# Slot-table rows of 512 instead of 64 bytes, with their first contents copied in halves from a block of 512 rows

## What is computed

```python
for k in range(TOP_K):
    y = _dispatch_compute(xf, top_experts[:, k], w1, w2, capacity)
    out = out + y * expert_weights[:, k][:, None]
```

## Time and profile before

| what | before |
|---|---|
| median of 3 executions | 2439.61 us (2436.92 to 2441.55) |
| the profiled execution | 2450.27 us |
| its span, first to last instruction | 2448.5 us |
| mean granted TensorE clock | 0.962 |
| busy: TensorE, VectorE, ScalarE, GpSimd | 90%, 55%, 41%, 47% |
| moved by DMA | 209.40 MB, 86 GB/s over the span |

### The profile page before, as it was taken

One profiled execution on the slowest core, in us unless ns is written; L12 is line 12 of the kernel. 1 busy time (PEld: TensorE's weight loads), 2 busy tenths in 40 slices (PEclk: granted clock), 3 DMA queues, 4 the chain that ended last, 5 costly groups with the idle time before them and its releaser, 6 DMA issues.

```text
span 2448.5 us, 57464 instructions
## 1 busy us (share of the span) xinstructions
PE 2204.8 (90%) x22468; PEld 1919.9 (78%) x22468; DVE 1344.1 (55%) x3312; ACT 1006.4 (41%) x2149; POOL 1142.9 (47%) x911
## 2 busy tenths in 40 slices
PE   6749998999999995999899999729999999999997
PEld 6738887999999995777677777628888899999997
DVE  7745443555555552578677786635444455555552
ACT  4433333444443442446545565423333344344442
POOL 4754766444444433223343333254677544444443
PEclk9999999999999998999999999859999999999999
DMA  8522433434344434101211111223333443433432
GB/s 334 209 72 47 92 73 81 80 96 100 79 97 85 92 75 112 34 24 72 72 38 55 55 72 56 71 78 80 77 79 76 96 98 81 100 78 96 98 82 29
DMA packets 129221, 209.40 MB, mean 86 GB/s; under 512 B 24876, under 2 KB 105328, under 8 KB 122864
## 3 DMA queue, kind: packets, MB, share of 16 engines
q0 software_dynamic: 57344, 69.21, 17.2%
q1 hardware_dynamic: 71696, 137.62, 16.3%
HBM read 136.03 MB, written 72.88 MB: 85 GB/s over the span
## 4 chain that ended last, share of the span: by engine, by line
PE 48%; DVE 4%; issue 3%; another core or an unknown queue 3%; ACT 1%; POOL 1%; DMA 1%; POOLq 0%; DVEq 0%; ACTq 0%
PE bank L630 15%; PE bank L641 14%; PE bank L714 9%; PE bank L802 3%; PE bank L835 1%; PE bank L770 1%; PE bank L619 1%; PE bank L785 1%; PE bank L874 1%; PE bank L820 1%; PE bank L732 1%; POOL slot_table L381 0%; DVE aw L1754 0%; DVE xnl L1728 0%
## 5 line engine op out<-in xcount | busy, mean ns | idle before, releaser
L1096 ACT ACTIVATE h<-bank 128x512 f32<-128x512 f32 x512 | 306.3, 598 | 934.2 <-PE bank L630 775.2
L1663 DVE CAST hh<-h 128x512 fp32r<-128x512 f32 x512 | 223.2, 436 | 776.3 <-ACT h L1096 670.7
L641 PE MATMUL bank<-w2h,hh 128*128 128x256 f32 x2048 | 586.3, 286 | 7.7 <-issue 7.4
L641 PE MATMUL bank<-w2l,hh 128*128 128x256 f32 x2048 | 582.7, 285 | 8.5 <-issue 8.3
L641 PE MATMUL bank<-w2h,hl 128*128 128x256 f32 x2048 | 582.7, 285 | 7.1 <-issue 6.8
L630 PE MATMUL bank<-xh,w1h 128*128 128x512 f32 x1024 | 412.7, 403 | 15.4 <-issue 9.2
L641 PEld LDWEIGHTS bank<-w2h,hh 128*128 128x128 f32 x2048 | 394.1, 192 | 30.1 <-issue 10.8
L641 PEld LDWEIGHTS bank<-w2l,hh 128*128 128x128 f32 x2048 | 394.5, 193 | 28.9 <-issue 11.7
L630 PE MATMUL bank<-xl,w1h 128*128 128x512 f32 x1024 | 409.6, 400 | 0.7 <-issue 0.6
L418 POOL DMA_INDIRECT xe<-xn_rows,tab x256 | 269.5, 1053 | 294.2 <-issue 261.8
L630 PE MATMUL bank<-xh,w1l 128*128 128x512 f32 x1024 | 403.8, 394 | 0.7 <-issue 0.6
(11 more groups left out here) (209 smaller groups left out, 3321.1 us busy)
## 6 DMA issues: line engine op xcount, KB each, us to landing
stg<-in_L_ffn_w SPq DMA_DIRECT2D x64, 1024.0 KB
xb<-acc SPq DMA_DIRECT2D x9, 1024.0 KB, 8.4
xa<-in_L_attn_x SPq DMA_DIRECT2D x8, 1024.0 KB, 14.0
xn_rows<-xa SPq DMA_DIRECT2D x8, 1024.0 KB
xn_rows<-xn_r SPq DMA_DIRECT2D x8, 1024.0 KB, 4.7
xr<-acc SPq DMA_DIRECT2D x7, 1024.0 KB, 5.4
out_rows<-xr SPq DMA_DIRECT2D x7, 1024.0 KB
slot_table<-pay,idx POOLq DMA_INDIRECT x256
```

The lines of the kernel that those rows point to most:

```text
L641: last = pe.matmul(o, a[:, fj, s], c[:, fj, :], start=(fj == 0 and n == 0 and t % 2 == 0), stop=(fj == FJ - 1 and n == 2), skip_group_chec ...
L1096: act.activation(h32[fj % 2][:], bank[fj % 2][:], ACT.Gelu_apprx_tanh).then_inc(f.gelu, 1)
L1663: dve.tensor_copy(hh[:, fj, :], h32[fj % 2][:]).then_inc(f.hh, 1)
```

## The change

A table row is 128 words (512 bytes). The scatter writes the whole row, so its window in `pay` is 128 words too, and the padding grows from 14 to 126 words per batch (the memset of L1596 from 112 to 1008 elements per partition). A table is 8 MB instead of 1. The input `slots_in` is now 512 such rows (256 KB), and a half of a table (the rows of one choice, 4 MB) is filled by one DMA whose source is that block, read 16 times. The first half of table 0 is issued behind the load of x of batch 3; its second half and both halves of table 1 stand in a row behind `normal_store(7)`, ahead of `ffn(0)`. GpSimd waits for the second half of table 0 behind the third gather, and for both halves of table 1 before attention. `tab` keeps two words per row, and the table loads fetch only these.

```diff
-        tab = sb("tab", [P, GE, GT, ROW])
+        tab = sb("tab", [P, GE, GT, 2])
...
+            def empty_slots(r, half, done):
+
+                rows = slot_d[r][half * (SLOTS // 2):(half + 1) * (SLOTS // 2), :].rearrange("(g s) w -> g s w", s=G)
+                sp.dma_start(rows, slots_in.unsqueeze(0).to_broadcast([NG // 2, G, ROW])).then_inc(done, 16)
+
             for b in range(1, B):
                 sp.dma_start(xa[:, b], x_w[b, :, :, :]).then_inc(X0[b], 16)
+                if b == 3:
+                    empty_slots(0, 0, S0.slot0)
...
             biased_store(1)
-            sp.dma_start(slot_d[0], slots_in).then_inc(S0.slot0, 16)
             biased_store(2)
...
             normal_store(7)
-            sp.dma_start(slot_d[1], slots_in).then_inc(S0.slot1, 16)
+            empty_slots(0, 1, S0.slot1)
+            empty_slots(1, 0, S0.slot2)
+            empty_slots(1, 1, S0.slot2)
...
-                tab_t = slot_d[r].rearrange("(g p t) w -> g p t w", p=P, t=GT)
+                tab_t = slot_d[r].rearrange("(g p t) w -> g p t w", p=P, t=GT)[:, :, :, 0:2]
...
                 gather(2, [(f.tab2, 16), (f.xT, 1)])
+                if r == 0:
+                    held(pool, S0.slot1, 16)
...
-            pool.wait_ge(S0.slot1, 16)
+            pool.wait_ge(S0.slot2, 32)
...
-ROW = 16
+ROW = 128
...
-    slots = np.zeros((SLOTS, ROW), np.uint32)
-    slots[:, 0] = N + np.arange(SLOTS) % G
+    slots = np.zeros((G, ROW), np.uint32)
+    slots[:, 0] = N + np.arange(G)
```

More of the change, by code:

```diff
@@ L174, in macaron_kernel @@
         nth = fill_numbers()
-        S0 = sems("setup", "const vec hvec rw zero acc_z out_z xn_z slot0 slot1 rope wraw wT wTh wTl bias memset base passed")
+        S0 = sems("setup", "const vec hvec rw zero acc_z out_z xn_z slot0 slot1 slot2 rope wraw wT wTh wTl bias memset base passed")
         X0 = [ctx.enter_context(nc.semaphore(f"first_x{b}")) for b in range(B)]
```

## The result

The kernel after the change takes 2462.6 us (median of 7 runs, 2452.94 to 2470.94); the kernel before, 2439.61 on the same chip (7 runs, 2421.72 to 2442.44). The ratio is 1.0101, 95% interval 1.0069 to 1.0134: slower by 17 to 33 us. The forecast was 2448.0, a loss of 8.4. The profiled execution of after is at its median (2462.6, span 2460.8), that of before stood 10.7 above its own, so the two traces differ by 12.3 us only.

The account below looks back on a forecast made before the run. TensorE, busy 90% of the span, was taken as the bound, with uncovered waits for gathered tokens at each expert stage's start. Copies 7.6 plus table loads 0.8 gave +8.4 us on the 2439.61 median: 2448.0, range 2395 to 2472.

Parts of the forecast that it names:

- Start-up copy: Table 0's first half, behind the fourth x load: lands near 28 us, gains and costs nothing; first `acc` store has 1.4 slack.
- Three copies ahead of the first table load: Behind `normal_store(7)`: 12.58 MB and queued scatters delay the first table load from 148.92 to 156.5, +7.6 us.
- 12 such pieces: 29.5 us: Ahead of the first expert stage: 12 pieces per ring at 2.46 us each occupy rings from 121.2 to 150.7.
- 20 x 0.23 = 4.6 us: Ring time of 20 scatters of batches 5 to 7 among the copies, half a gather each; rings clear at 155.3.
- The rule that spoke against the change: Trainium skill's 214 GB/s for HBM-to-HBM copies: the three copies before the first expert stage take 59 us, sum near +38.
- Table loads, +0.8: 512 pieces of 8 bytes instead of 128 of 256 add 0.4 us to the first load of either expert stage.
- the other loads lie a whole token group ahead of use: Inside the expert stages: table loads after each stage's first are early enough that narrowing them adds nothing.
- Scatter issue: GpSimd's issue time per scatter hardly depends on row size: 0 taken, between 0 and 0.1 us each.
- the moved wait: GpSimd's wait for the other half after the third gather, and its round-1 wait, find copies long landed: nothing.
- The third rival: Scatters' small writes stretch token groups and attention, some 108 us; whole rows could free part, half giving 2394. Chance 0.24.
- The slow copy: Long shared-source copies run at half rate: 29.5 us more at expert start, 8.4 at the `acc` store, 2486. Chance 0.12.
- The hidden copy: Scatters stay at 0.06 us per ring, table load 4.2 us late; total 2442 to 2445. Chance 0.12.

Follow-up runs that it names:

- the narrow loads alone: Kernel before with only its table loads changed, to two words of each 64-byte row: ratio 1.0091 on chip C, 1.0019 on chip D.
- long source, narrow loads: Changed kernel, each copy reading its own 4 MB input of 8192 rows once instead of 256 KB 16 times: ratio 1.0076 against before.
- scatters of 64 bytes, narrow loads: Changed kernel with 512-byte rows and long copies, but scatters writing only the first 16 words of a row: ratio 1.0082 against before.
- copies spread, narrow loads: Changed kernel, table 0's second half copied behind `normal_store(3)`, table 1's halves in the middle of the first expert stage: ratio 1.0081 against before.
- quarters spread, narrow loads: Changed kernel, table 0's second half cut in four between stores before the first expert stage, table 1 in quarters during attention: ratio 1.0069 against before.
- copies alone, whole loads: Kernel before plus three 4.19 MB copies into tensors nobody reads, behind the copy of table 1: ratio 1.0091 on B, 1.0087 on D.

## Why the prediction was right in direction and short in size

The time of 2462.6 us lies in the stated range (2395 to 2472), but 4.6 above the 2458 at which the forecast's own bounds ended. The path was the predicted one; two terms of the sum were too small.

**Start-up copy, costed at nothing: right.** It landed at 29.4 us (4.38 + 25.0; forecast near 28), `ln_rs` moved to 29.55, nothing earlier came of it. The first `acc` store took longer than its forecast of 40 us, and the slack of 1.4 us at it was used up: VectorE's row of after, against 41.44 in the earlier trace rows,

```profile
42.36 2.29 DVE L1623 TENSOR_TENSOR xr<-xa,hbias 128x2048 f32<-128x2048 f32 x1 [0.38 <-DMA acc<-xr]
```

waits 0.38 us for it, and the last scatter is 0.43 us later; the copies ahead of the table load cover that. Up to 38 us the rings moved 346 GB/s instead of 373 at nearly the same share (0.94 and 0.93), with this copy among their traffic.

**Three copies ahead of the first table load: the failed step.** The mechanism is the predicted one: 12 pieces per ring, the last scatters behind them because a ring turns to the other queue once per packet, and the table load behind these scatters. The term was mis-sized. "12 such pieces: 29.5 us" took some 40 (121.5 to about 161.5, forecast 150.7), because the 2.46 us of the earlier trace rows hold for the first piece on each ring only; later ones take 3.34. "20 x 0.23 = 4.6 us" for the scatters was about 2, for another reason than bytes: 436 packets that had been given no turn. Then some 1.2 us to the load, as forecast. That makes 15.6 us where 7.6 stood; by luck the scatters' term, too large by 2.7, hid a part of the 10.5 that the copies' term was short. Both spread runs show that the delay belongs to the copies at that place: without them there the load is at 148.9.

The rule that spoke against the change, 214 GB/s at full rate for copies of tiles of 128 x 16 KiB between HBM tensors (the Trainium skill, DMA: Bandwidth & Descriptors, Latency and other measured facts), named the right danger and the wrong size for these copies. The 12.6 MB went in 40 us, 315 GB/s, which lies between it and the 426 I used. The Trainium skill also states (same page, Queues, rings and completion order) that a DMA engine turns between its queues after each packet. The trace agrees, with 64 packets of either queue from 132 to 142 us, and what follows is that large pieces on one queue set the pace of the other.

**Table loads, +0.8: right at the place that was costed, too small for the kernel.** Load to gather is 3.06 us instead of 2.55 at the first expert stage (164.53 to 167.59) and 3.04 instead of 2.53 at the second: +1.0 together. But the narrow loads alone cost 3.0 us by medians on D (2.3 to 6.6) and 20 on C. The forecast's "the other loads lie a whole token group ahead of use", which put them at nothing, may be the place, and no run shows it.

**Scatter issue and the moved wait, 0: right.** The page of after, part 5, against the earlier trace rows:

```profile
L389 POOL DMA_INDIRECT slot_table<-pay,idx x256 | 265.7, 1038 | 114.4 <-issue 94.5
```

**The sum.** Start 15.6 and table loads 1.0 are 16.6 us, just under the interval of the ratio (17 to 33) and 6.4 under the medians' 23.0. With the 3.0 us of chip D for the narrow loads it is 18.6. On the chips without stalls these two terms are nearly all. By medians:

| run | chip | late or lost at the named place | whole loss | rest |
|---|---|---|---|---|
| long source, narrow loads | B | 14.5 (first table load) | 17.9 | 3.4 |
| scatters of 64 bytes, narrow loads | B | 15.9 (first table load) | 19.9 | 4.0 |
| copies spread, narrow loads | B | 15.3 (two groups) | 18.0 | 2.7 |
| quarters spread, narrow loads | D | 10.5 (attention) | 13.5 | 3.0 |
| copies alone, whole loads | B | 19.0 (first table load) | 20.6 | 1.6 |
| copies alone, whole loads | D | 18.6 (first table load) | 20.2 | 1.6 |

A place is read in one trace: the first table load against 148.91 on B and 149.32 on D, the two groups against even ones, attention against the narrow loads alone. Each rest alone is within the interval of its ratio; but it is 2.7 to 4.0 us wherever the loads are narrow. On A 4.4 us are left beyond 18.6, on C 7.5 beyond 16.4 and 3.0. The narrow loads may hold them, since alone they cost 20 us on C; but the change, which has them and the copies, costs 27 there and not 40. No run separates them.

**The third rival (small writes stretch the groups, 0.24): fallen, though its pool is real.** I had priced it at 37 + 31 + 40 = 108 us. Chips B and D, with the very same kernel before, are 100 us faster than A, and the three places are those: eight groups in 187.5 us instead of 224.8 in the first stage and 218.9 in the second, and from the last group of the first stage to the second stage's first gather 639 to 644 us (seven kernels, all but the quarters) instead of 682.8. The "remote" waits are not there. Of the 37 us in the first stage TensorE is idle for 19.5 and busy for 17.8 more, at a mean granted clock of 0.95 instead of 1.00. But on A eight groups went only from 224.80 to 216.41 and from 218.86 to 218.18 with whole rows, in one execution each; on C from 226.5 to 224.8 and from 225.1 to 234.0. In attention the six waits of ScalarE stand as they did (before, after, on A):

```profile
ACT vz L1188 <- remote: 40.0, 6, 7.3
```

```profile
ACT vz L1198 <- remote: 39.5, 6, 7.1
```

**The slow copy (0.12)** came true by a third: it wanted 59 us for the three copies, they took 40 and not 29.5. **The hidden copy (0.12)** fell with the load at 164.5.

## What to carry to other kernels

A copy that nobody waits for is not free while its queue is first in, first out: what its ring time exceeds the slack by, it costs to the next load that somebody does wait for. Here 12.6 MB, 40 us on the rings, cost 15.6 us ahead of the first expert stage, 8.4 MB cost 15 in its middle and about 10 in attention. Take the rate for such a copy from a stretch of full rings with the same two ends, not from the first piece of a burst; and mind the size of the pieces, because another queue on the same rings gets one packet per piece. Cutting a load down to the bytes in use isn't free either: 3.0 us on D. Before rows are widened so that writes are large, check that the small ones cost anything: here 8, 64 and 512 bytes made no difference on the chips on which that was measured.

## What the runs showed of the hardware

- The same kernel takes 2337 to 2339 us on two chips and 2440 to 2457 on two others. The difference lies in waits that the profile marks "remote", while GpSimd issues eight scatters and four gathers in a row, and six scatters in attention: ScalarE and VectorE then wait together, and TensorE goes on with gaps marked "issue". On the fast chips these waits are absent. What makes them was not found.
- Copies from HBM to HBM: 2.47 us for the first 64 KB piece on each ring, 3.34 in the long run with a shared source of 256 KB, 3.11 with one of 4 MB. From SBUF to HBM in 2 KB pieces, 348 to 369 GB/s.
- Rings with work of two queues took their packets one for one, whatever their size: 64 and 64 in 10 us, up to 64 KB on one side and 2 KB on the other.
- With full rings, TensorE stood still 5.05 us in attention without a named wait, instead of 1.48, and a 16 KB packet of the instruction queue came 4 us later. Whether the one makes the other was not tried.
